# Graph layers on one core: one step's rows in every eighth batch come by 128 plain DMAs from SyncE instead of one gather from GpSimd

## What is computed

```python
h = jnp.maximum(_layernorm(x, axis=-1), 0.0)
x = x + _L0_gnn_ref(h, edge_index, ...)   # e = sum(q[dst] * k[src]) / 4, softmax by dst,
                                          # agg = segment_sum(alpha * v[src], dst), then FFN
h = jnp.maximum(_layernorm(x, axis=-1), 0.0)
x = x + _L1_gnn_ref(h, src, dst, ...)     # neigh = segment_sum(feat[src], dst)
                                          # relu((feat + neigh) @ W1 + b1) @ W2 + b2
```

## Time and profile before

| | |
|---|---|
| time, median of 3 runs | 4823.37 us |
| the profiled execution's own time | 4832.58 us |
| its span | 4830.8 us |
| POOL busy | 3417.5 us, 71% of the span |
| DVE busy | 2764.8 us, 57% |
| ACT busy | 2158.4 us, 45% |
| PE busy | 475.0 us, 10% |
| DMA, mean over the span | 169 GB/s |

### The profile page before, as it was taken

One profiled execution on the slowest core, in us unless ns is written; L12 is line 12 of the kernel. 1 busy time (PEld: TensorE's weight loads), 2 busy tenths in 40 slices (PEclk: granted clock), 3 DMA queues, 4 the chain that ended last, 5 costly groups with the idle time before them and its releaser, 6 DMA issues.

```text
span 4830.8 us, 22063 instructions
## 1 busy us (share of the span) xinstructions
PE 475.0 (10%) x2377; PEld 333.0 (7%) x2377; DVE 2764.8 (57%) x4386; ACT 2158.4 (45%) x2237; POOL 3417.5 (71%) x3610
## 2 busy tenths in 40 slices
PE   3420000000000000000189100000000000000007
PEld 2310000000000000000067000000000000000004
DVE  7647988898889898888778222222222222222223
ACT  3314554454444555545367344444444444444432
POOL 4577777777777777777554677777777777777766
PEclk8765555555555555555589555555555555555558
DMA  9995666666666666666455333333333333333334
GB/s 357 384 369 194 216 210 210 214 212 211 209 213 213 214 214 215 214 213 213 141 115 126 94 102 100 100 106 102 104 104 104 104 104 104 104 104 104 104 98 140
DMA packets 235480, 816.44 MB, mean 169 GB/s; under 512 B 67005, under 2 KB 93789, under 8 KB 185242
## 3 DMA queue, kind: packets, MB, share of 16 engines
q0 software_dynamic: 143232, 344.58, 25.4%
q1 hardware_dynamic: 77464, 457.58, 24.9%
q10 hardware_dynamic: 14722, 13.70, 0.8%
HBM read 455.00 MB, written 354.21 MB: 168 GB/s over the span
## 4 chain that ended last, share of the span: by engine, by line
POOL 59%; issue 25%; DMA 8%; PE 5%; DVE 2%; ACT 1%; SPq 0%; POOLq 0%; ACTq 0%; DVEq 0%
POOL arena L635 58%; DMA q_edges<-arena 7%; PE ps L1291 2%; PE ps L1302 2%; DMA arena<-states,node_idx 1%; PE ps L1323 0%; DVE arena L1728 0%; ACT arena L1130 0%; PE ps L1282 0%; SPq L532 0%; POOLq L122 0%; PE ps L1315 0%; DVE arena L1955 0%; DMA states<-arena 0%; POOL q_edges L639 0%
## 5 line engine op out<-in xcount | busy, mean ns | idle before, releaser
L635 POOL DMA_INDIRECT arena<-h_tab,idx x1568 | 1483.4, 946 | 520.6 <-issue 501.6
L635 POOL DMA_INDIRECT arena<-kv_tab,idx x1568 | 1487.4, 949 | 502.5 <-issue 501.6
L1904 DVE SCALAR_TENSOR_TENSOR ps<-arena,keep,ps 128x128 f32<-128x128 f32 x97 | 42.5, 438 | 1487.6 <-ACT ps L1179 1487.6
L1179 ACT COPY ps<-arena 128x2048 f32<-128x2048 f32 x97 | 348.0, 3588 | 941.0 <-DMA arena<-h_tab,idx 941.0
L1076 ACT COPY arena<-arena 128x1024 f32<-128x1024 f32 x196 | 375.7, 1917 | 549.7 <-DVE arena L1728 549.7
L1612 DVE TENSOR_TENSOR_SCAN ps<-arena,ps 128x256 f32<-128x256 f32 (+2 forms) x584 | 502.6, 861 | 0.1
L1186 ACT COPY arena<-arena 128x1024 f32<-128x1024 f32 x196 | 379.0, 1934 | 212.2 <-DVE arena L1912 210.6
L1728 DVE TENSOR_TENSOR_SCAN arena<-arena,ps 128x1024 f32<-128x1024 f32 x196 | 443.1, 2261 | 0.1
L1912 DVE TENSOR_TENSOR_SCAN arena<-arena,ps 128x1024 f32<-128x1024 f32 x194 | 433.1, 2274 | 10.3 <-DVE ps L1904 0.5
L1042 ACT COPY ps<-arena 128x1024 f32<-128x1024 f32 x196 | 363.5, 1887 | 10.0 <-DMA arena<-q_edges 4.0
L1664 DVE TENSOR_TENSOR arena<-arena,ps 128x1024 f32<-128x1024 f32 x196 | 230.5, 1218 | 180.8 <-DMA arena<-kv_tab,idx 180.8
(11 more groups left out here) (248 smaller groups left out, 2379.0 us busy)
## 6 DMA issues: line engine op xcount, KB each, us to landing
states<-arena SPq DMA_DIRECT2D x98, 1152.0 KB, 5.4
q_edges<-arena SPq DMA_DIRECT2D x98, 1024.0 KB, 6.1
arena<-q_edges SPq DMA_DIRECT2D x98, 1024.0 KB, 7.8
states<-arena SPq DMA_DIRECT2D x98, 1024.0 KB, 4.1
arena<-kv_tab,idx POOLq DMA_INDIRECT x1568, 2.8
arena<-h_tab,idx POOLq DMA_INDIRECT x1568, 2.5
kv_tab<-arena ACTq DMA_DIRECT2D x14, 896.0 KB, 11.2
arena<-kv_tab SPq DMA_DIRECT2D x14, 448.0 KB, 5.3
```

Source lines behind the costliest of these rows:

```text
L635: pool.indirect_dma_start(to, None, tab, bass.IndirectOffsetOnAxis(ap=at, axis=0)).then_inc(done, 16)
L1179: nc.scalar.copy(rows_now, rows[k].rearrange("p b f -> p f b")).then_inc(rows_turned, 1)
```

## The change

In every eighth batch (batches 9, 17, ..., 97, twelve of them, all with k = 1) the last of the 16 steps is no longer gathered by POOL, in both passes. SP fetches its 128 rows by 128 DMAs, each of one row to one partition, whose address comes from a register, into a new buffer (`direct_kv`, `direct_h`). Twenty at most (19 in pass D) are issued in each of the batches before. When all have landed and `kvb[1]` (`rows[1]`) is free, one DMA copies the buffer into its column. The row numbers come from a small table `direct_tab` in device memory (12 x 128), which stage A makes from `src_all` by a strided copy, a matmul with the identity and a copy back. SP loads up to 20 of them into registers at a time. To hold the pattern, SP, POOL and ACT (in pass D) now loop over eight batches, with the first eight and the last two written out. Some semaphores of the node passes are shared to make room; their waits are otherwise the same.

```diff
+OCTETS = BATCHES // 8
+DIRECT_AT = 9 * B + B - 1
+ROWS_B = (0, 8) + (20,) * 6
+ROWS_D = (19, 19) + (18,) * 5 + (0,)
@@ SP, ahead of pass B @@
+            sp.wait_ge(prep, PREP_LIST)
+            sp.dma_start(direct_tab, direct_rows[0:OCTETS, :]).then_inc(direct_listed, 16)
@@ SP @@
+            def row_numbers(o, by_slot, r):
+
+                if not by_slot[r]:
+                    return []
+                p0 = sum(by_slot[0:r])
+                return nc.values_load_multi_w_load_instructions(
+                    direct_tab[bass.ds(o, 1), p0:p0 + by_slot[r]], engines=[mybir.EngineType.SP], min_val=0, max_val=N - 1,
+                    skip_runtime_bounds_check_because="edges name nodes")[1]
+
+            def fetch(to, tab, numbers, p0, done):
+
+                for p, number in enumerate(numbers, p0):
+                    sp.dma_start(to[p:p + 1, :], tab[bass.ds(number, 1), :]).then_inc(done, 16)
+
+            def slot_b(o, r, first):
+
+                n, k = o * 8 + r, r % 2
+                if not last_batch(n):
+                    if not (first and r == 0):
+                        sp.wait_ge(q_turned, n * 2)
+                        settle(sp)
+                    sp.dma_start(qb[1 - k], q_rows[:, bass.ds(n * B + B, B), :]).then_inc(q_in[1 - k], 16)
+                filling = not (isinstance(o, int) and o == OCTETS)
+                numbers = row_numbers(o, ROWS_B, r) if filling else []
+                p0, ahead = sum(ROWS_B[0:r]), len(numbers) // 2 if r > 1 else 0
+                fetch(direct_kv, kv_tab, numbers[0:ahead], p0, direct_kv_in)
+                if not (first and r == 0):
+                    store_b(n - 1, 1 - k)
+                if r == 0 and not first:
+                    sp.wait_ge(direct_kv_in, o * 16 * P)
+                    sp.wait_ge(weighed_s, n * 2)
+                    settle(sp)
+                    sp.dma_start(kvb[1][:, B - 1, :], direct_kv).then_inc(direct_set, 16)
+                if r == 1 and not first and filling:
+                    sp.wait_ge(direct_set, o * 16)
+                    settle(sp)
+                fetch(direct_kv, kv_tab, numbers[ahead:], p0 + ahead, direct_kv_in)
@@ SP, pass D @@
+            def slot_d(o, r, first):
+
+                n, k = o * 8 + r, r % 2
+                filling = not (isinstance(o, int) and o == OCTETS)
+                numbers = row_numbers(o, ROWS_D, r) if filling else []
+                sp.wait_ge(sums_set, n + 1)
+                settle(sp)
+                sp.dma_start(by_step(states1)[:, bass.ds(n * B, B), :], sums_b[k]).then_inc(sums_out[k], 16)
+                if r == 0 and not first and filling:
+                    sp.wait_ge(direct_set, (OCTETS + o) * 16)
                     settle(sp)
+                fetch(direct_h, h2_tab, numbers, sum(ROWS_D[0:r]), direct_h_in)
+                if r == 7:
+                    sp.wait_ge(direct_h_in, o * 16 * P + 16 * P)
+                    sp.wait_ge(rows_turned, n + 1)
+                    settle(sp)
+                    sp.dma_start(rows[1][:, B - 1, :], direct_h).then_inc(direct_set, 16)
@@ POOL, both passes (pass B shown) @@
-                    for b in range(B):
-                        gather(kvb[k][:, b, :], kv_tab, idx[k][:, b:b + 1], kv_in[k])
-            repeat(pool, BPAIRS, batch_b)
+                for b in range(B if first or r != 1 else B - 1):
+                    gather(kvb[k][:, b, :], kv_tab, idx[k][:, b:b + 1], kv_in[k])
+            octets(pool, slot_b)
@@ PE and DVE, end of stage A @@
+            pe.wait_ge(prep, PREP_COLUMNS)
+            nc.tensor.matmul(ps[0:OCTETS, 5, 0:P], direct_cols, ident[:], start=True, stop=True).then_inc(direct_ps, 1)
+            step(nc.vector.tensor_copy(direct_cols, src_all[:, DIRECT_AT:STEPS:8 * B]))
+            dve.wait_ge(direct_ps, 1)
+            step(nc.vector.tensor_copy(direct_rows[0:OCTETS, :], ps[0:OCTETS, 5, 0:P]))
@@ DVE, pass B @@
-                dve.wait_ge(kv_in[k], n // 2 * BW + BW)
+                dve.wait_ge(kv_in[k], n // 2 * BW + BW - 16 * k * (n // 8))
+                if n % 8 == 1 and n > 8:
+                    dve.wait_ge(direct_set, n // 8 * 16)
```

More of the change, by code:

```diff
@@ L57 @@
 EREST = E - EFULL * STEPS
+OCTETS = BATCHES // 8
+DIRECT_AT = 9 * B + B - 1
+ROWS_B = (0, 8) + (20,) * 6
+ROWS_D = (19, 19) + (18,) * 5 + (0,)
+assert BATCHES == 8 * OCTETS + 2 and sum(ROWS_B) == P and sum(ROWS_D) == P
 BPAIRS = BATCHES // 2
@@ L317, in build @@
         disorder = cA.take(1).bitcast(I32)
+        direct_cols = cA.take(OCTETS)
+        direct_rows = cA.take(P).bitcast(I32)
         cS = Carve(arena)
@@ L499, in build, with octets @@
         GWAIT = 16 * G
+        def octets(eng, slot):
+            for r in range(8):
+                slot(0, r, True)
+            with eng.Fori(1, OCTETS) as o:
+                for r in range(8):
+                    slot(o, r, False)
+            for r in range(2):
+                slot(OCTETS, r, False)
         def settle(eng):
@@ L868, in _, with slot_b @@
             first_rows(EARLY_ROWS + 2, B)
[L870 to L878, removed]
-                    for b in range(B):
-                        gather(kvb[k][:, b, :], kv_tab, idx[k][:, b:b + 1], kv_in[k])
-            repeat(pool, BPAIRS, batch_b)
+            def slot_b(o, r, first):
+                n, k = o * 8 + r, r % 2
+                if first and r == 0:
+                    return
+                pool.wait_ge(idx_set, n + 1)
+                if not (first and r < 2):
+                    pool.wait_ge(weighed_s, (n - 1) * 2)
+                settle(pool)
+                for b in range(B if first or r != 1 else B - 1):
+                    gather(kvb[k][:, b, :], kv_tab, idx[k][:, b:b + 1], kv_in[k])
+            octets(pool, slot_b)
             for k in range(2):
@@ L930, in _, with slot_d @@
                 pool.wait_ge(h2_stored[k], 16 * PAIRS)
[L932 to L941, removed]
+            def slot_d(o, r, first):
+                n, k = o * 8 + r, r % 2
+                pool.wait_ge(idx1_set, n + 1)
+                if not (first and r < 2):
+                    pool.wait_ge(rows_turned, n - 1)
+                settle(pool)
+                for b in range(B if first or r != 1 else B - 1):
+                    gather(rows[k][:, b, :], h2_tab, idx[k][:, b:b + 1], rows_in[k])
+            octets(pool, slot_d)
             for k in range(2):
@@ L1166, in _ @@
             keep1_features(0, 0)
[L1168 to L1182, removed]
-                        act.wait_ge(sums_out[k], i * 16)
-                    for half in range(2):
-                        act.wait_ge(sum_s, n * 2 + half + 2)
-                        done = nc.scalar.copy(sums_b[k][:, :, half * HF:(half + 1) * HF].rearrange("p b f -> p f b"),
-                                              run_sums[:, half * HF * B:(half + 1) * HF * B].rearrange("p (f b) -> p f b", b=B))
-                    done.then_inc(sums_set, 1)
```

73 lines of the change are left out of this document (44 added, 29 removed).

## The result

| | before | after |
|---|---|---|
| median | 4823.89 us (4820.99 to 4825.84, 4 runs) | 4768.40 us (4766.73 to 4773.67, 4 runs) |
| profiled execution, its span | 4832.58, 4830.8 us | 4773.67, 4771.7 us |

The ratio is 0.9888 (0.9876 to 0.9900): 55 us faster, where 30 were forecast.

What follows compares the result with a forecast made beforehand. POOL was taken to bound the kernel: 12 x 1.269 + 12 x 1.266 = 30.4 us of gathers removed, the additions hidden, so 4823.4 - 30.4 = 4793.0 us for the median, range 4786 to 4812.

Steps and rivals of the forecast that it cites:

- What bounds, what is removed: POOL bounds both passes; twelve gathers fewer in each save 30.4 us, and DVE and ACT let all of it through.
- With these gaps a gather costs 1.269 us: POOL's busy plus "issue" time over 1568 gathers: 1.269 us each in pass B, 1.266 in pass D.
- longer gap now and then: On POOL between gathers: occasionally 2.05 us instead of 0.30, counted into the cost of each gather.
- SP's fetches: Row fetches at a register address on SP: 0.50 us each, between 0.39 and 0.61; 64 us for 128 rows.
- A list value: SP's load of row numbers into registers: 0.3 us a value, 6 us for twenty.
- A pointer: SP's pointer load ahead of each portion of fetches: 1.0 us, as POOL's single-value load.
- batch of 18.4 us: SP's time for a batch with 20 fetches, 10 + 1 + 6 + 1.4, of 20.3 us: SP keeps up.
- The query load: On SP behind ten fetches: leaves about 5 us later, takes 7.8 us to land, with 9 us left.
- The copy: From the new buffer into kvb[1]: 2.8 us, as a gather's landing, hidden in about 19 us.
- The stall at each turn of the longer loop: Rival: POOL refetches instructions at each turn back, 10 times a pass, 2.0 us each: 40 us, 4833 us; 8 in 100.
- The fetches slow the gathers: Rival: fetch completions disturb POOL's gathers, 1% on each of 3112: 39 us, 4832 us; 3 in 100.
- SP becomes the bound: Rival: loading row numbers makes SP late; at 0.7 us a value 166 us more, 4989 us; 12 in 100.

Runs made afterwards that it cites:

- e3: Changed kernel, but SP fetches and copies into spare rows nobody reads, and POOL gathers all 16 steps of every batch: 4822.53 us, ratio 1.0000 to the kernel before.
- e1: Changed kernel with its octet loops but without SP's fetches and copies, POOL gathering all 16 steps of every batch: 4822.32 us, ratio 0.9998 to the kernel before.

## Why the prediction was wrong, point by point

- *What bounds, what is removed*: right. L699 has x1556, nobody waits anew, and the 24 gathers are worth 24 x 1.25 = 30.0 us. DVE's wait ahead of its first product fell in batches 9, 17 and so on from 1.6 to 0.2 to 0.3 us, by the 1.3 that was named as a sign; of the 0.6 us of room that the forecast gave it there, about half is left.
- **The step that failed** is "With these gaps a gather costs 1.269 us", and with it the range's "gaps that go with the gathers". The "longer gap now and then" was spread evenly over 1568 gathers and taken as a property of each. It is a periodic stop of 2 us, tied to the count of gathers and the start of a batch, 48.1 us of both passes, and the one gather less in eight batches more than halved it: 27 us. The forecast said 30.4, the POOL rows say 30.0 + 27.2 = 57, the clock 55. Of the forecast's 30.4 only 0.4 goes beyond the gathers' plain spacing, where the stops gave 27.
- *SP's fetches* at 0.50 us: measured 0.39 and 0.51. *A list value* at 0.3: measured 0.14 in pass B and 0.42 in pass D (medians of lists of 20 and of 18), so the one term stood between two, and pass D was nearer to the 0.61 us from which SP falls behind than forecast. The Trainium skill ("Runtime: NRT & Kernel Launch", "Instruction fetch mechanics") gives some 0.2 us a register; the trace is below that in B and at twice it in D. *A pointer* at 1.0: 2.5 in B, 1.1 in D. The forecast's batch of 18.4 us leaves 1.9; in pass B 5.1 were left.
- *The query load* lands in 5.4 us, not 7.8, and had its room. *The copy* lands in 4.8 us, not 2.8 (L615, 4.1/4.8/5.6), hidden in its 19 us. e3 shows both at nothing.
- *The stall at each turn of the longer loop*: refuted for POOL, whose gathers have no longer distance in either pass beyond those told above. The instruction packets, 54 before and 192 after, are SP's loop, and hidden there on this chip.
- *The fetches slow the gathers*: refuted, e3 is at 1.0000, and a gather is busy 944 to 946 ns there as in e1.
- *SP becomes the bound*: not here, with more room than thought; on two other chips yes, in variants of the changed kernel. The rival's price of a value (from 0.51 us on) was the wrong gauge: what failed there is most instructions of SP, at 0.7 us or more for stretches.
- *Not accounted for*: in the kernels with gathers left out the part behind the last gather takes 171 to 172 us, in the others on the faster chips 165 to 167. That stays open.

## What to carry to other kernels

A mean gap is a sum of kinds. Before pricing "n fewer of these", list the gaps that differ from the rest with their positions: if they are periodic, the change may move the period and be worth double, or nothing; here 24 gathers more were 13 us faster. The same holds for a median over both passes: the loads of row numbers are 2.9 us in one and 7.5 in the other. And work that is moved to an idle engine's queue can meet a chip on which that engine is slow: a gain of 1.1% on one chip stood against a loss of 22 to 24% on two others, for almost the same program. I would keep this change only where the chip is known.

## What the runs showed of the hardware

- POOL's chain of indirect DMAs stops every 112 gathers of 128 rows by 2.0 us (pass B) or 1.8 us (pass D), if that count falls behind the first gather of a batch; by 0.8 or 0.6 us behind the second, then 111 apart. A kernel with 17 gathers in each eighth batch has no stop in pass B and one in D.
- In either place the stop ends 3.3 us (pass B) or 3.1 us (pass D) after the batch's first gather started.
- A register load of 20 values from device memory takes 2.8 us on SP in pass B, one of 18 values 7.5 us in pass D (medians); one of a single value 2.5 and 1.1.
- SP's loop with the fetches takes 133 packets of 8 KB more of instructions than the same loop without them, and loses no time by it here.
- Chips differ, as far as one visit to each can tell: on three of five (those with 5337 to 5365 us for the kernel before) SP's instructions take 0.7 us or 1.4 us for stretches, on the other two register operations never exceed 0.1.
